# Storing and loading K and Q as whole rows, with both copies of K's high part in one load

## The reference

```
qh, kh, vh = split(layernorm(x) @ wq + bq), split(ctx @ wk + bk), split(ctx @ wv + bv)
attn = softmax(qh @ kh.T / sqrt(16))
x = x + tanh(g_xattn) * ((attn @ vh) @ wo + bo)
x = x + tanh(g_ffn) * (gelu(layernorm(x) @ w1 + b1) @ w2 + b2) * sum(normalised top-2 router weights)
```

## Time and profile before

| | |
|---|---|
| three runs | 732.95, 734.27 (median), 735.4 us |
| the profiled execution | 734.14 us |
| its span, first to last instruction | 732.1 us |
| granted TensorE clock, mean | 0.991 |

### The profile page before, as it was taken

How to read it: one execution, slowest core, us unless ns; L and a number is a source line. 1 busy time by engine, 2 the same in 40 slices (tenths; PEclk the granted TensorE clock), 3 DMA queues, 4 the chain that set the end, 5 groups by cost and what they waited for, 6 DMA issues and landing times.

```text
span 732.1 us, 20618 instructions
## 1 busy us (share of the span) xinstructions
PE 696.4 (95%) x7648; PEld 652.3 (89%) x7648; DVE 514.4 (70%) x1298; ACT 402.5 (55%) x800; POOL 321.3 (44%) x476
## 2 busy tenths in 40 slices
PE   3688999999999999999999999999999999999987
PEld 2566888999999999999999999999999999988966
DVE  6378788777776777776777777777677777766422
ACT  2124666465564646556564746556474655656753
POOL 4313436444434545434344544343454543424246
PEclk9979999999999999999999999999999999999999
DMA  4868789866748585764658486684758576450000
GB/s 146 179 198 169 187 189 224 155 170 137 178 104 174 125 187 132 171 167 124 158 111 206 103 187 154 129 190 110 165 122 182 139 171 150 104 93 3 15 1 27
DMA packets 84021, 103.21 MB, mean 141 GB/s; under 512 B 9589, under 2 KB 79570, under 8 KB 83922
## 3 DMA queue, kind: packets, MB, share of 16 engines
q1 hardware_dynamic: 83282, 101.12, 59.9%
q10 hardware_dynamic: 640, 0.77, 0.5%
HBM read 65.05 MB, written 34.05 MB: 135 GB/s over the span
## 4 chain that ended last, share of the span: by engine, by line
PE 87%; DVE 4%; ACT 2%; issue 2%; POOL 2%; SPq 1%; DMA 1%; ACTq 0%; POOLq 0%; DVEq 0%
PE P L921 42%; PE S L951 13%; PE T L963 11%; PE OT L978 11%; PE P L1004 4%; PE TR L987 2%; PE TR L1060 1%; DVE NEGM L764 1%; PE TR L1043 1%; ACT PROBS L678 1%; PE TR L994 1%; PE TR L936 1%; DVE XN L832 1%; PE TR L1028 1%; DMA QS<-q_parts 1%
## 5 line engine op out<-in xcount | busy, mean ns | idle before, releaser
L764 DVE TENSOR_REDUCE NEGM<-S 112x1 f32<-112x375 f32 x512 | 267.3, 539 | 73.4 <-PE S L951 71.3
L678 ACT ACTIVATE PROBS<-T 125x448 f32<-125x448 f32 x384 | 196.2, 543 | 106.0 <-PE T L963 98.4
L951 PE MATMUL S<-KS,QS 96*112 96x376 f32 x512 | 181.7, 361 | 9.6 <-DVE NEGM L764 6.3
L963 PE MATMUL T<-QS,KS 98*125 98x224 f32 x768 | 150.6, 282 | 3.1 <-ACT PROBS L678 1.7
L963 PEld LDWEIGHTS T<-QS,KS 98*125 98x125 f32 x768 | 129.3, 188 | 10.0 <-ACT PROBS L678 4.6
L582 POOL CAST HT_HI<-HG 128x224 fp32r<-128x224 f32 x128 | 47.3, 369 | 152.0 <-ACT HG L701 144.0
L951 PEld LDWEIGHTS S<-KS,QS 96*112 96x112 f32 x512 | 91.3, 180 | 23.5 <-DVE NEGM L764 13.0
L566 POOL CAST CT_HI<-CTRAW 128x750 fp32r<-128x750 f32 x31 | 25.1, 810 | 161.7 <-DMA CTRAW<-in_ctxT 151.0
L584 POOL TENSOR_TENSOR HT_LO<-HG,HT_HI 128x224 fp32r<-128x224 f32 x128 | 85.2, 666 | 10.3
L978 PE MATMUL OT<-PROBS,VA 125*17 125x112 f32 x3072 | 87.6, 260 | 0.0
L701 ACT ACTIVATE HG<-P,B 128x224 f32<-128x224 f32 x128 | 57.2, 447 | 53.4 <-PE P L921 52.2
(11 more groups left out here) (113 smaller groups left out, 1496.8 us busy)
## 6 DMA issues: line engine op xcount, KB each, us to landing
KS<-k_parts SPq DMA_DIRECT2D x90, 375.0 KB, 7.1
CTRAW<-in_ctxT SPq DMA_DIRECT2D x32, 375.0 KB, 3.5
k_parts<-KHI SPq DMA_DIRECT2D x30, 375.0 KB, 3.9
k_parts<-KLO SPq DMA_DIRECT2D x30, 375.0 KB, 4.5
QS<-q_parts SPq DMA_DIRECT2D x96, 112.0 KB, 4.9
X<-in_x SPq DMA_DIRECT2D x16, 224.0 KB, 3.6
q_parts<-QHI SPq DMA_DIRECT2D x32, 112.0 KB, 2.4
q_parts<-QLO SPq DMA_DIRECT2D x32, 112.0 KB, 2.3
```

Source lines behind the costliest of these rows:

```text
L678: act.activation(PT[0:KN, k, pp * 4 * SQ:(pp + 1) * 4 * SQ], T_BANK[i % 2][0:KN, 0:4 * SQ], ACT.Exp, scale=SCALE).then_inc(exp_done, 1)
L764: dve.tensor_reduce(NEGM[:, b.par, i:i + 1], S_BANK[i % 2][0:SQ, 0:SK], AX.X, ALU.max, negate=True).then_inc(max_done, 1)
L951: pe.matmul(S_BANK[i % 2][0:SQ, 0:SKP], QS[0:96, i, b.ring * SQ:(b.ring + 1) * SQ], KS[0:96, b.ring, i // 2, :], start=True, stop=True).th ...
L963: mm = pe.matmul(T_BANK[i % 2][0:KN, r * 2 * SQ:(r + 1) * 2 * SQ], KS[0:98, prv.ring, pair, k * KN:(k + 1) * KN], QS[0:98, 2 * pair:2 * pa ...
```

## The change

DRAM's `k_parts` and `q_parts` are laid out by partition row, with all eight pairs side by side in each row (width 376 for K, 224 for Q), so that one row is contiguous. `KHI` and `KLO` become 376 wide. A store now writes 3008 bytes per source partition (K) or 1792 (Q), and its DRAM side runs over 4, then 32 (or 16) rows, then the run. A load of K's low part is 32 rows of 12,032 bytes. K's high part is loaded into partitions 32 to 95 by one transfer, whose source is a broadcast of two copies of 32 rows; the low part moves to partitions 0 to 31. `QS` is laid out so that a load writes 7168 contiguous bytes in a partition. Pairs stand in another order, which `head()`, the columns of `NEGM` and the rows of `WO` follow. Stages and their order are the same (in `kd`, only the numbers are swapped with the rows).

```diff
-        QS = sb("QS", [128, NH, RING * SQ], F32R)
-        KHI = sb("KHI", [128, DC, SK], F32R)
-        KLO = sb("KLO", [128, DC, SK], F32R)
+        QS = sb("QS", [128, 2, 2, NPAIR, TOK], F32R)
+        KHI = sb("KHI", [128, DC, SKP], F32R)
+        KLO = sb("KLO", [128, DC, SKP], F32R)
...
-        KD = nc.dram_tensor("k_parts", (2, 2, NPAIR, 32, SK), F32, kind="Internal").ap()
-        QD = nc.dram_tensor("q_parts", (2, 2, DC, 4, DH, TOK), F32, kind="Internal").ap()
+        KD = nc.dram_tensor("k_parts", (2, 2, 32, NPAIR * SKP), F32, kind="Internal").ap()
+        QD = nc.dram_tensor("q_parts", (2, 2, DH, NPAIR * TOK), F32, kind="Internal").ap()
...
         def loads_of(b):
-            return 48 * ((b.k - DIRECT) // 2 + 1)
+            return 32 * ((b.k - DIRECT) // 2 + 1)
+        def head(h):
+            return 2 * NPAIR // DC * (h // 2 % DC) + 2 * (h // 2 // DC) + h % 2
...
-                        sp.dma_start(QS[r0:r0 + DH, hh:NH:2, cols].bitcast(F32),
-                                     QD[part, hh].rearrange("c p r n -> r (c p) n")).then_inc(qs_loaded, 16)
+                        sp.dma_start(QS[r0:r0 + DH, g.gpar, hh, :, :].bitcast(F32),
+                                     QD[part, hh].rearrange("r (g n) -> r g n", g=NPAIR)).then_inc(qs_loaded, 16)
...
-                        sp.dma_start(QS[96:97, :, cols].bitcast(F32), MHI[:, :].bitcast(F32)).then_inc(m_loaded, 16)
+                        sp.dma_start(QS[96:97, prv.gpar, :, :, cols].bitcast(F32), MHI[:, :].bitcast(F32)).then_inc(m_loaded, 16)
...
-                        sp.dma_start(KD[nn.par, 0].rearrange("(c p) r n -> (p r) c n", c=DC),
+                        sp.dma_start(KD[nn.par, 0].rearrange("r (p n) -> p r n", p=4),
                                      KHI[:, :, :].bitcast(F32)).then_inc(khi_stored, 16)
...
-                        for row in (0, 2):
-                            sp.dma_start(KS[32 * row:32 * row + 32, nn.ring, :, 0:SK].bitcast(F32),
-                                         KD[nn.par, 0].rearrange("g r n -> r g n")).then_inc(ks_loaded[nn.par], 16)
+                        sp.dma_start(KS[32:96, nn.ring, :, :].rearrange("p g n -> p (g n)").bitcast(F32),
+                                     KD[nn.par, 0].unsqueeze(0).to_broadcast([2, 32, NPAIR * SKP])
+                                     ).then_inc(ks_loaded[nn.par], 16)
                         held(sp, sp_passed, (klo_stored, stored))
-                        sp.dma_start(KS[32:64, nn.ring, :, 0:SK].bitcast(F32),
-                                     KD[nn.par, 1].rearrange("g r n -> r g n")).then_inc(ks_loaded[nn.par], 16)
+                        sp.dma_start(KS[0:32, nn.ring, :, :].rearrange("p g n -> p (g n)").bitcast(F32),
+                                     KD[nn.par, 1]).then_inc(ks_loaded[nn.par], 16)
...
-                            sp.dma_start(QD[0, hh].rearrange("c p r n -> (p r) c n"),
+                            sp.dma_start(QD[0, hh].rearrange("r (p n) -> p r n", p=4),
                                          QHI[64 * hh:64 * hh + 64, :, :].bitcast(F32)).then_inc(qhi_stored, 16)
```

More of the change, by code:

```diff
@@ L83 @@
     (-3, """"""),
-    (-2, """cl+1 xl-2 l1 xn cx ct wk k.0 wv k.1 wq xt ka.2 l1-2 kd.1 q.0 q.1 qs v.0 cl v.1 xn-2 tg v.2 v.0-1
-       v.1-1 kd.0 ct-1"""),
+    (-2, """cl+1 xl-2 l1 xn cx ct wk k.0 wv k.1 wq xt ka.2 l1-2 kd.0 q.0 q.1 qs v.0 cl v.1 xn-2 tg v.2 v.0-1
+       v.1-1 kd.1 ct-1"""),
     (-1, """k.0 k.1 xt-1 v.2"""),
-    (0, """s.0 s.1 s.2 s.3 s.4 ql+1 kd.1+1 s.5 kd.0+1 s.6 s.7 ka.2+1 s.8 lw2.0 s.9 s.10 s.11 lw1 q.0 on+1 s.12
+    (0, """s.0 s.1 s.2 s.3 s.4 ql+1 kd.0+1 s.5 kd.1+1 s.6 s.7 ka.2+1 s.8 lw2.0 s.9 s.10 s.11 lw1 q.0 on+1 s.12
        s.13 ct q.1 s.14 s.15 k.0"""),
@@ L374, in build @@
         N_PROJ = 1 + 2
-        N_REST = 1 + 2 + 2
+        N_REST = 1 + 2 + 1 + 4
         TURNED = TR[:, 0:DC * TOK].rearrange("p (c n) -> p c n", c=DC)
@@ L392, in loads_of @@
         def loads_of(b):
-            return 48 * ((b.k - DIRECT) // 2 + 1)
+            return 32 * ((b.k - DIRECT) // 2 + 1)
+        def head(h):
+            return 2 * NPAIR // DC * (h // 2 % DC) + 2 * (h // 2 // DC) + h % 2
         def move_k(engine, b, row):
-            part, moved = (KLO, klo_moved) if row == 1 else (KHI, khi_moved)
+            part, moved = (KLO, klo_moved) if row == 0 else (KHI, khi_moved)
             for p in range(4):
-                engine.dma_start(KS[32 * row:32 * row + 32, b.ring, p:NPAIR:4, 0:SK].bitcast(F32),
+                engine.dma_start(KS[32 * row:32 * row + 32, b.ring, DC * p:DC * (p + 1), :].bitcast(F32),
                                  part[32 * p:32 * p + 32, :, :].bitcast(F32)).then_inc(moved[b.k], 16)
@@ L436, in stack_q @@
             def stack_q(g):
-                cols = slice(GB * g.gpar * SQ, GB * (g.gpar + 1) * SQ)
                 for row, part in ((0, 0), (1, 0), (2, 1)):
@@ L461, in step @@
                         load(B2[:, :], b2.partition_broadcast(SQ), rest_loaded)
-                        for dst, src in ((WO, wo), (WR, wr)):
-                            load(dst[:, :, :], src.rearrange("(c p) n -> p c n", p=128), rest_loaded)
+                        load(WR[:, :, :], wr.rearrange("(c p) n -> p c n", p=128), rest_loaded)
+                        for i in range(2):
+                            for c in range(DC):
+                                load(WO[64 * i + 32 * c:64 * i + 32 * c + 32, :, :],
+                                     wo[128 * c + 32 * i:128 * c + 32 * i + 96].rearrange("(k r) n -> r k n", r=32)[:, 0:3:2, :],
+                                     rest_loaded)
                     if op == "m" and prv.exists:
-                        cols = slice(prv.ring * SQ, (prv.ring + 1) * SQ)
+                        cols = slice(prv.j * SQ, (prv.j + 1) * SQ)
                         held(sp, sp_passed, (mhi_done, prv.count(1, 1)))
-                        sp.dma_start(QS[96:97, :, cols].bitcast(F32), MHI[:, :].bitcast(F32)).then_inc(m_loaded, 16)
+                        sp.dma_start(QS[96:97, prv.gpar, :, :, cols].bitcast(F32), MHI[:, :].bitcast(F32)).then_inc(m_loaded, 16)
                         held(sp, sp_passed, (mlo_done, prv.count(1, 1)))
-                        sp.dma_start(QS[97:98, :, cols].bitcast(F32), MLO[:, :].bitcast(F32)).then_inc(m_loaded, 16)
+                        sp.dma_start(QS[97:98, prv.gpar, :, :, cols].bitcast(F32), MLO[:, :].bitcast(F32)).then_inc(m_loaded, 16)
                     if op == "ql" and nxt.exists:
@@ L479, in step @@
                     if op == "kd":
-                        held(sp, sp_passed, (klo_done if i == 1 else khi_done, nn.count(2, 2)))
+                        held(sp, sp_passed, (klo_done if i == 0 else khi_done, nn.count(2, 2)))
                         move_k(sp, nn, i)
                     if op == "ks" and nn.exists:
-                        held(sp, sp_passed, (ks_loaded[nn.par], loads_of(nn) - 48), (khi_done, nn.count(2, 2)))
-                        sp.dma_start(KD[nn.par, 0].rearrange("(c p) r n -> (p r) c n", c=DC),
+                        held(sp, sp_passed, (ks_loaded[nn.par], loads_of(nn) - 32), (khi_done, nn.count(2, 2)))
+                        sp.dma_start(KD[nn.par, 0].rearrange("r (p n) -> p r n", p=4),
                                      KHI[:, :, :].bitcast(F32)).then_inc(khi_stored, 16)
                         held(sp, sp_passed, (klo_done, nn.count(2, 2)))
-                        sp.dma_start(KD[nn.par, 1].rearrange("(c p) r n -> (p r) c n", c=DC),
+                        sp.dma_start(KD[nn.par, 1].rearrange("r (p n) -> p r n", p=4),
                                      KLO[:, :, :].bitcast(F32)).then_inc(klo_stored, 16)
@@ L513, in step @@
                         for hh in range(2):
-                            sp.dma_start(QD[1, hh].rearrange("c p r n -> (p r) c n"),
+                            sp.dma_start(QD[1, hh].rearrange("r (p n) -> p r n", p=4),
                                          QLO[64 * hh:64 * hh + 64, :, :].bitcast(F32)).then_inc(qlo_stored, 16)
@@ L533, in _ @@
             pool.memset(VA[:, :, :, :, DH:VW], 1.0).then_inc(pool_zeroed, 1)
-            pool.memset(QS[:, 0:NH // 2, :].bitcast(F32), 0.0).then_inc(pool_zeroed, 1)
+            pool.memset(QS[:, 0, :, :, :].bitcast(F32), 0.0).then_inc(pool_zeroed, 1)
             pool.memset(IDENT[:, :], 0.0).then_inc(ident_done, 1)
@@ L632, in step @@
                     if op == "ka":
-                        act.wait_ge(klo_done if i == 1 else khi_done, nn.count(2, 2))
+                        act.wait_ge(klo_done if i == 0 else khi_done, nn.count(2, 2))
                         move_k(act, nn, i)
@@ L653, in step @@
                             act.wait_ge(khi_stored, nn.count(16, -16 * DIRECT))
-                        act.activation(KHI[:, i, :], bank[:, 0:SK], ACT.Identity,
+                        act.activation(KHI[:, i, :], bank[:, 0:SKP], ACT.Identity,
                                        bias=BK[:, i:i + 1]).then_inc(khi_done, 1)
```

(13 more changed lines are left out.)

## The result

The changed kernel takes 1051.0 us, median of four runs (1043.8 to 1054.2), against 734.4 for the kernel before: 1.430 times, 95% interval 1.422 to 1.438. The forecast was 945, in 850 to 1140. The profiled execution took 1050.4 us.

The account below looks back on a forecast made before the run. The first two DMA engines were to become the bound, 56.4 us a period against PE's 41.75. Fourteen periods of 14.65 (205), less 4, plus 6.7 and 3 for gaps, gave +211 on 734.1: 945 us, range 850 to 1140.

Parts of the forecast that it names:

- PE the bound before, gain at most 3.4 us: Kernel before: PE busy 696.4 of 732.1 us, so editing transfers can give back at most 3.4 us of DMA waits.
- The spread: Transfers are cut into equal shares by outermost count: K's high load on 2 engines, K and Q stores on 4.
- Prices: Confined K and Q transfers run at 25.6 GB/s per engine: high load 15.0 us, K store 3.8, Q store 1.12.
- the first engine's sum: Work of the first DMA engine, which shares in every transfer: 56.4 us per period against 41.75 us of PE time.
- Where it reaches PE: Delays enter PE at `st.0`, which waits for the maxima; the loop closes at 56.4 us a period.
- the late one is the maxima: In `st.0` the maxima land late, 6.7 us and then 8.0 more; K and Q loads are in time.
- the first engine never idles: In the steady state the first DMA engine works without a gap through the whole 56.4 us period.
- The start and the ends: First period costs 4 less, the half period after the last Q store adds 6.7; 3 us for gaps between transfers.
- the Q store at 45.6: Store, called the third, from which the loop was taken to hold for 14 periods of 14.65 us extra, 205 us.
- PE's clock: Clock may fall around PE's stalls, but stays covered by the first engine's work: nothing added, up to 4 us a period in range.
- The second: Rival: only K's high load is confined, the stores are not; first engine 41.7 us a period, 742 us; chance 0.04.
- The third: Rival: long rows run slowly, at 14.5 GB/s; high load 26.6 us, period 79.5, time 1263 us; chance 0.06.
- The first: Rival: transfers spread over all 16 engines whatever their outermost count; 730.7 to 734.1, say 733 us; chance 0.08.

Follow-up runs that it names:

- e6: Changed kernel with DRAM laid out by (p, row) and K loaded by three transfers, all outermost counts multiples of 16: 734.3 us, ratio 0.9996 to the kernel before.
- e5: Kernel of e6, but K's high part stored twice as 64 real rows and loaded by one transfer over 64 partitions: 735.5 us, ratio 0.9994.
- e1: Changed kernel with K's high part loaded by two transfers of 32 partitions, stores still with 4 slices outermost: 823.0 us, ratio 1.119.
- h8: Changed kernel with only Q's transfers back on 16 engines, stores as 64 rows in one slice: 1044.5 us, ratio 1.419.
- g1: Changed kernel with 48 filler products on PE ahead of each wait for the maxima: 1069.1 us, ratio 1.456.
- h1: Kernel of e2 with Q's stores also as 64 rows in one slice, so only the high load is confined: 919.3 us, ratio 1.248.
- e2: Changed kernel with each K store made as four transfers of 32 partitions, high load unchanged: 927.0 us, ratio 1.260.
- h3: Kernel before with only the maxima's two loads issued by ACT in place of SP: 760.6 us, ratio 1.033.

## Why the prediction was right, and where it was not

**PE the bound before, gain at most 3.4 us.** Right: e6 and e5, with long rows and no confinement, are at 0.9996 and 0.9994.

**The spread.** Right, and shown: equal shares by the outermost count, 2 engines for the high load, 4 for the stores. Landing times missing, shares of 0.13 and 0.25, and e5 against the changed kernel. The completion steps that the trace holds say the same: 150 for the 30 stores of K's high part, five each, where the kernel before has 480; 160 for the 32 Q stores of one part, five each, where it has 512; 285 for 15 high loads and 15 low loads, three and 16 a pair. That is one more than the slices each time. The rule quoted from the Trainium skill ("DMA: Bandwidth & Descriptors", "Rules for kernel authors") holds here to the number: a broadcast of two, two engines. The sign follows from this step and the prices.

**Prices.** The high load was right (25.0 GB/s an engine). K's and Q's stores took longer than priced: two stores of K with all four engines at work run at 99/(16 x 0.26) = 23.8 GB/s in the changed kernel and at 110/(16 x 0.31) = 22.2 in e1, Q's at 70/(16 x 0.27) = 16.2 in e1, not 25.6 (the first window is the changed kernel's, the others are e1's):

```profile
526.90:528.90 2.00, 2.00 (x17) 1.92 (x16) 1.88 (x7) 0.79 (x3) 1.92 (x3) 1.00 0.26 99
```
```profile
416.20:418.80 2.60, 2.60 (x60) 2.42 (x55) 1.02 (x4) 1.84 (x3) 0.00 (x0) 1.00 0.31 110
391.00:394.50 3.50, 3.50 (x43) 3.23 (x46) 2.74 (x8) 1.96 (x4) 0.00 (x0) 1.00 0.27 70
```

A K store is then 4.0 to 4.3 us an engine in place of 3.8. Why the stores are slower was not tested. With two high loads at 25.0 GB/s (30.8 us) the first engine's sum becomes 58 to 62 us a period in place of 56.4, the low end with Q's stores as the prediction had them.

**Where it reaches PE.** This step failed in part. It had "the late one is the maxima" and closed the loop by the first engine's sum, 56.4. The first `st.0` was placed at 13.7 and came at 12.8 (521.29, from 508.46), but for another reason: it waited only 0.2 us for the maxima, since PE had stood 3.8 us for DVE and the bank before. The second maxima cost PE 11.9 us, where 8.0 had been given. But the output store was followed to 64.0 in the queue and then dropped: I did not ask who waits for it. DVE does, in `wo`, and through the bank PE, before `k.1`; so K's next stores are issued 8.9 to 11.7 us after the Q store, mostly about 11, not 5.7. With SP's wait for the low store ahead of the output store, that is the chain of 61.3.

The prediction's "the first engine never idles" does hold for the changed kernel, nearly, and its sum at measured prices, 58 to 62, meets the period too. But h8 takes some of that work away, its engines do stand idle, and the period stays at 61.8: the chain is a bound by itself. That the two lie within a few us of each other the prediction did not see, and that 56.4 came close to 61.3 was luck in this respect. Whether the sum would hold the period near 61 if the chain were cut no run shows. In the middle the miss is 4.9 us in each of eleven periods, 52 us.

**The start and the ends.** Another 44 us of the miss are in the second to fourth periods: 211.0 us against 123.0 before, +88, where three times 14.65 had been given. There PE waits 19.9 us in two waits for `KS` itself, and SP stands 14.1 us in the issue of one load of weights (from 72.72); what each is worth was not separated. With the clock at 0.84 in place of 0.75 there (g1) the stretch was as long. The tail took 113.0 against 103.2, the start to the second Q store 5.0 more; the ends together are 9 us above what was given for them. (The prediction calls the Q store at 45.6 the third; it is the second, and its 14 periods are counted rightly.) 88 + 213.6 + 9.8 + 5.0 = 316.4, where 213.6 is the middle, 673.9 against 460.3 before.

**PE's clock.** Right that it falls (0.87 in the middle, with the lower level, 1.2 GHz, in windows where PE stands, as 553 to 555) and right that the stalls cover it there (g1). For the periods before the middle this is not shown.

**Rivals.** The second, only the high load confined, was priced at 742 and is h1: 919. It had the same fault, a sum in place of the queue's order and SP's waits. The third fell: long rows run at 25 GB/s. The first fell with the landing times.

## What to carry to other kernels

Look at the outermost count on both sides of each DMA before anything else: a broadcast or a split put outermost can take a transfer from 16 engines to 2, which the profile shows as a missing landing time and a DMA share of 0.13. To price it, don't stop at the slow engine's sum: everything issued behind the slow transfer lands after it, so list each small transfer behind it with its waiter, and look for a closed chain through SP's own waits. The view of waits names what PE feels and the chain what bounds; here they named different things. Filling the longest wait gained nothing (g1), and spreading K's stores, which stand in the chain, gained 124 us (e2).

## What the runs showed of the hardware

- SP stood 10.26 us in the issue of one x load, behind a high load and two stores that were not done, and 9.9 us at the median of 14 such issues (0.35 before). In h1 and e2, with the same high load but K's stores on 16 engines, the median was 0.33 us; in e1, with the stores on 4 engines but no such load, 1.7. So slow transfers together can also hold the issuing engine, with all that is behind it in its order.
- Two small DMAs a batch on ACT in place of SP, with ACT's waits for the data that they move, cost 25 us in 32 batches (h3), 0.8 us a batch, in a kernel where ACT is 55% busy.
- One transfer of 752 KB over 64 partitions, on 16 engines, lands in 6.2 us at the median (e5), as long as each of three of 376 KB over 32 partitions in the same 12,032-byte rows (e1); in 3008-byte rows these take 6.9 (e6).
